# Deformable sampling on one core: one of a step's 72 gathered columns is fetched by SyncE, pixel by pixel

## The reference

```python
offsets = _conv_same(xi, off_w[g], off_b[g])
offsets = offsets.reshape(B, H, W, K * K, 2)
loc = grid[None, :, :, None, :] + kg[None, None, None] + offsets
...
out = wa[..., None] * gather(y0i, x0i) + wb[..., None] * gather(y1i, x0i) + wc[..., None] * gather(y0i, x1i) + wd[..., None] * gather(y1i, x1i)
```

## Time and profile before

| | us |
|---|---|
| three executions, median (lowest, highest) | 12371.41 (12371.2, 12372.86) |
| profiled execution, its own time | 12375.1 |
| its span, first to last instruction | 12373.3 |
| GpSimd busy | 8754.7 (71%) |
| TensorE matmul busy | 7826.9 (63%) |
| VectorE busy | 5178.4 (42%) |
| ScalarE busy | 1654.1 (13%) |
| gathers of GpSimd | 9216 |

### The profile page before, as it was taken

One profiled execution on the slowest core, in us unless ns is written; L12 is line 12 of the kernel. 1 busy time (PEld: TensorE's weight loads), 2 busy tenths in 40 slices (PEclk: granted clock), 3 DMA queues, 4 the chain that ended last, 5 costly groups with the idle time before them and its releaser, 6 DMA issues.

```text
span 12373.3 us, 133594 instructions
## 1 busy us (share of the span) xinstructions
PE 7826.9 (63%) x46178; PEld 6378.0 (52%) x46178; DVE 5178.4 (42%) x6138; ACT 1654.1 (13%) x2837; POOL 8754.7 (71%) x9269
## 2 busy tenths in 40 slices
PE   5766667666467765554457775655457776655488
PEld 3554455545457644444447654444446664444474
DVE  3344444443344444343344444343344444344333
ACT  1011111110011112110001111210001111211015
POOL 3777777777777777777777777777777777777700
PEclk8887778877678877776678877777678887877689
DMA  2333334333244422432234422332224432343271
GB/s 86 102 88 97 111 89 111 105 94 102 73 125 160 130 66 78 115 95 61 67 102 146 167 68 71 100 110 71 57 80 146 171 93 64 92 112 91 62 248 56
DMA packets 878254, 1255.70 MB, mean 101 GB/s; under 512 B 183384, under 2 KB 663320, under 8 KB 860248
## 3 DMA queue, kind: packets, MB, share of 16 engines
q0 software_dynamic: 294912, 604.57, 19.2%
q1 hardware_dynamic: 512216, 601.04, 14.4%
q10 hardware_dynamic: 70912, 47.20, 1.2%
HBM read 1069.49 MB, written 245.50 MB: 106 GB/s over the span
## 4 chain that ended last, share of the span: by engine, by line
POOL 68%; issue 23%; PE 4%; DVE 1%; DMA 1%; ACT 0%; POOLq 0%; PEld 0%; SPq 0%; PEldq 0%; ACTq 0%; DVEq 0%
POOL gathered L471 68%; PE stage L1033 2%; PE stage L926 1%; DVE srow L1561 0%; DMA gathered<-table,idx 0%; PE acc L926 0%; DVE gathered L1554 0%; PE pt L926 0%; POOLq L469 0%; PE wtb L926 0%; PE acc L1175 0%; PEld acc L1175 0%; PE stage L988 0%; POOLq L467 0%; POOLq L477 0%
## 5 line engine op out<-in xcount | busy, mean ns | idle before, releaser
L471 POOL DMA_INDIRECT gathered<-table,idx x9216 | 8730.2, 947 | 2979.2 <-issue 2801.6
L1175 PE MATMUL acc<-stt,room 128*128 128x128 f32 (+1 forms) x30600 | 4372.0, 308 | 234.6 <-ACT stt L901 234.6
L1175 PEld LDWEIGHTS acc<-stt,room 128*128 128x128 f32 (+1 forms) x30600 | 4220.1, 221 | 543.5 <-ACT stt L901 341.5
L1164 PE MATMUL pt<-mat,srow 128*128 128x128 f32 x2048 | 507.2, 394 | 3682.6 <-DVE srow L1561 3682.2
L1164 PEld LDWEIGHTS pt<-mat,srow 128*128 128x128 f32 x2048 | 327.5, 196 | 3882.9 <-DVE srow L1561 3870.6
L1530 DVE COPY idx<-idxn 128x18 uint32<-128x18 uint32 x512 | 98.1, 192 | 5195.8 <-DMA gathered<-table,idx 5187.5
L1561 DVE TENSOR_REDUCE srow<-gathered 128x576 f32<-128x2304 f32 x512 | 2081.1, 4065 | 0.1
L1554 DVE TENSOR_TENSOR gathered<-gathered,wtb 128x2304 f32<-128x2304 f32 x512 | 1306.1, 2551 | 63.0 <-DMA gathered<-table,idx 62.6
L901 ACT ACTIVATE stt<-pt 128x512 f32<-128x512 f32 x512 | 305.9, 597 | 5968.0 <-PE pt L1164 5965.6
L926 PE MATMUL stage<-room,mat 128*128 128x512 f32 (+1 forms) x1360 | 791.4, 712 | 296.6 <-DVE room L1425 70.8
L1033 PE MATMUL stage<-room 128*128 128x128 f32 x7680 | 890.2, 278 | 12.8 <-DMA room<-toep 10.6
(11 more groups left out here) (206 smaller groups left out, 3931.7 us busy)
## 6 DMA issues: line engine op xcount, KB each, us to landing
gathered<-table,idx POOLq DMA_INDIRECT x9216
room<-toep SPq DMA_DIRECT2D x64, 1792.0 KB, 19.0
room<-toep SPq DMA_DIRECT2D x64, 1280.0 KB, 11.5
room<-toep SPq DMA_DIRECT2D x64, 768.0 KB
table<-room SPq DMA_DIRECT2D x64, 512.0 KB, 2.9
toep<-in_taps SPq DMA_DIRECT2D x128, 224.0 KB
toep<-in_taps SPq DMA_DIRECT2D x128, 160.0 KB
room<-in_x SPq DMA_DIRECT2D x4, 4096.0 KB
```

The lines of the kernel that those rows point to most:

```text
L471: nc.gpsimd.indirect_dma_start(gat[r][:, k % K9 * G + k // K9, :], None, table[b].rearrange("(n e) -> n e", e=PAIR), bass.IndirectOffsetOn ...
L1164: ins = nc.tensor.transpose(pt[:, m, :], srow[r % 2][:, m * P:(m + 1) * P], M["ident"])
L1175: ins = nc.tensor.matmul(acc[a][:, 0:W], wk[0:kk, m, dx, block_at * C:block_at * C + P], stt[s][0:kk, m, dx:dx + W], start=start and m == ...
```

## The change

One column of the 72, row `AT_R` = 0 and sample `AT_K` = 17, is no longer gathered by GpSimd, except in step 0. VectorE scales this column's 128 indices to addresses in words and writes them to a tile `column` of 128 x 1 integers. SyncE stores it to DRAM (`column_d`), waits for that, waits until row 0 of the current step is summed, and then fetches the 128 pixels of the next step in 8 chunks of 16: it reads 16 registers from `column_d`, and issues 16 plain DMAs, each of one partition and 128 words, with the register as source address. The chunks stand at times spread over the step, at 1, 2.5, 4 and so on to 11.5. VectorE waits for all 128 of them (`pixels_in`) beside the 17 gathers before it treats row 0. A few semaphores that nothing waited for are dropped as well, and `next_image` drains VectorE where it waited for its own semaphore.

```diff
+AT_R, AT_K = 0, GK - 1
+CHUNK = 16
...
+        column_d = nc.dram_tensor("column_d", [STEPS, P], I32).ap()
...
+        column = sb("column", [P, 1], I32)
...
+        def pixel(p):
+
+            return gat[AT_R][p:p + 1, AT_K % K9 * G + AT_K // K9, :]
...
                 def step(n, b):
                     for r in range(ROWS):
                         v = n * ROWS + r
+                        own = GK if r != AT_R or isinstance(n, int) else AT_K
                         pool.wait_ge(idx_given, v + 1)
                         pool.wait_ge(summed, v + 1)
                         pool.sem_inc(started, 1)
-                        for k in range(GK):
+                        for k in range(own):
...
+                regs = [sp.alloc_register(f"at{j}") for j in range(CHUNK)]
+
+                def fetch_column(n):
+
+                    sp.wait_ge(column_given, n)
+                    sp.dma_start(column_d[ds(n, 1), :].rearrange("o p -> p o"), column[:]).then_inc(column_out, 16)
+                    sp.wait_ge(column_out, 16 * n)
+                    sp.sem_inc(started, 1)
+
+                def fetch_pixels(n, b, q):
+
+                    sp.load(regs, column_d[ds(n, 1), CHUNK * q:CHUNK * (q + 1)])
+                    for j in range(CHUNK):
+                        at = sp.snap(regs[j], min_val=0, max_val=(NPAIR - 2) * PAIR)
+                        sp.dma_start(pixel(CHUNK * q + j), table[b][ds(at, ENTRY)].unsqueeze(0)).then_inc(pixels_in, 16)
+
...
-                    if b == 0:
-                        for k in range(ROWS):
-                            yield 3 * k + 1
+                    last = isinstance(n, int) and n == STEPS - 1
+                    for k in range(ROWS):
+                        yield 3 * k + 1
+                        if b == 0:
                             bands(ROWS * i + k)
+                        if last:
+                            continue
+                        if k == 0:
+                            fetch_column(n + 1)
+                            sp.wait_ge(summed, n * ROWS + AT_R + 1 + ROWS)
+                            sp.sem_inc(started, 1)
+                        per = P // CHUNK // ROWS
+                        for q in range(per * k, per * (k + 1)):
+                            yield 3 * k + 1 + 3 * (q % per) / per
+                            fetch_pixels(n + 1, nb, q)
...
                     then(tt(idxn[:], entry, gbase[:], ALU.add))
+                    if not (isinstance(n, int) and n == 0):
+                        if not (isinstance(n, int) and n == 1):
+                            dve.wait_ge(column_out, 16 * n - 16)
+                        ts(column[:], idxn[:, AT_R, AT_K:AT_K + 1], float(PAIR), None, ALU.mult).then_inc(column_given, 1)
...
-                    dve.wait_ge(landed[r], 16 * GK * (n + 1))
+                    dve.wait_ge(landed[r], 16 * GK + 16 * (AT_K if r == AT_R else GK) * n)
+                    if r == AT_R and not (isinstance(n, int) and n == 0):
+                        dve.wait_ge(pixels_in, 16 * P * n)
                     if give:
                         give_indices(v, r)
```

More of the change, by code:

```diff
@@ L371, in build @@
         table_out = sems("table_out0", "table_out1")
-        off_in, off_used, chain, idx_given, wt_given, moved, started = sems(
-            "off_in", "off_used", "chain", "idx_given", "wt_given", "moved", "started")
+        off_in, off_used, chain, idx_given, wt_given, started = sems(
+            "off_in", "off_used", "chain", "idx_given", "wt_given", "started")
+        column_given, column_out, pixels_in = sems("column_given", "column_out", "pixels_in")
         landed = sems(*(f"landed{r}" for r in range(ROWS)))
@@ L380, in build @@
         bands_out = sems(*(f"bands_out{l}" for l in range(3)))
-        folded, shift_p, ctx_p, gate_p, ctx_s, gate_s = sems("folded", "shift_p", "ctx_p", "gate_p", "ctx_s", "gate_s")
+        shift_p, ctx_p, gate_p, ctx_s, gate_s = sems("shift_p", "ctx_p", "gate_p", "ctx_s", "gate_s")
         cx_out = sems(*(f"cx_out{u}" for u in range(4)))
@@ L474, in step @@
                                 .then_inc(landed[r], 16)
+                step(0, 0)
                 for b in range(NB):
-                    with pool.Fori(b * PER, (b + 1) * PER) as n:
+                    with pool.Fori(max(b * PER, 1), (b + 1) * PER) as n:
                         step(n, b)
@@ L1357, in context_fold @@
                     scale(S["wq"], M["wq"])
-                    scale(gws[:], gw[:]).then_inc(folded, 1)
+                    scale(gws[:], gw[:])
                     yield 13
@@ L1362, in context_fold @@
                     tt(b_q2, PB[2][:, 1:2], V["b_q"], ALU.add)
-                    tt(b_gate2[0:8, :], PB[2][0:8, 2:3], b_gate, ALU.add).then_inc(folded, 1)
+                    tt(b_gate2[0:8, :], PB[2][0:8, 2:3], b_gate, ALU.add)
                 def operands_fold(b, i):
                     yield 11
-                    scale(S["ccen"], M["ccen"]).then_inc(folded, 1)
+                    scale(S["ccen"], M["ccen"])
                     yield 13
                     dve.wait_ge(shift_p, 2 * b + 2)
-                    nc.vector.tensor_copy(b_cen, PB[2][:, 0:1]).then_inc(folded, 1)
+                    nc.vector.tensor_copy(b_cen, PB[2][:, 0:1])
                 def context(b, i):
@@ L1565, in next_image @@
                 def next_image(b):
-                    nc.vector.tensor_copy(base[:], base0[:]).then_inc(moved, 1)
-                    dve.wait_ge(moved, b + 1)
+                    nc.vector.tensor_copy(base[:], base0[:])
+                    dve.drain()
                 def start():
```

## The result

The changed kernel takes 14400.61 us (median of four executions, 14395.13 to 14409.41), the kernel before 12372.01 on the same chip: a ratio of 1.164, with a 95% interval of 1.1625 to 1.1655. It is slower by 2029 us; 14,570 was forecast.

The account below looks back on a forecast made before the run. GpSimd's gathers bound the kernel before, at 90.3 us a step; SyncE's copies, reads and waits would bound the changed one. 12375 + 778 + 1834 - 354 - 56 = 14577, so 14,570 us, range 13,000 to 15,900.

Parts of the forecast that it names:

- What bounds the kernel, and the worth of the gather: GpSimd's gathers bound the kernel before; one gather fewer in each of 127 steps takes off 159 us.
- SyncE becomes the bound, and GpSimd waits for it through VectorE's indices: SyncE's step of 114.6 us in image 0, 109.6 after, exceeds GpSimd's 89.05 and holds VectorE, then GpSimd; 56%.
- A copy at 0.48 us: Each one-pixel copy on SyncE, with register arithmetic, move and boundaries, takes 0.48 us; 128 take 61.4 us a step.
- One memory answer for each read: Each SyncE read, of pointer or 16 words, takes 1.7 us: 27.2 us a looped step, 13.6 in the others.
- The stretch without pixels, 16 us: Each step, SyncE fetches no pixel for 16 us while offsets load, indices are made and row 0 is summed.
- SyncE keeps up: Rival: the column's fetch fits into GpSimd's 89.05 us step, GpSimd stays the bound, 12216 us, about 12,230; 12%.
- One memory answer a chunk: Rival: SyncE's pointer reads are nearly free, so pixels take 75 us a step and the time is 13,200 us; 15%.
- The DMA engine is the limit: Rival: one-partition copies use a single DMA engine and back up; at 0.6 us a copy 16,500 us; 16% with dearer reads.
- the ring: Not in the prediction; later reading: pixels, their row, other engines' work behind it, SyncE's stores for them, the next pixels.

Follow-up runs that it names:

- experiment 3: The changed kernel with 17 gathers in row 0 and no column work on SyncE, the column's samples left out: 12215.72 us, ratio 0.9872.
- experiment 1: The changed kernel with the 16 registers read only once, before the first pixels, and all copies kept: 12220.01 us, ratio 0.9876.
- experiment 7: The changed kernel with a column of row 3 instead of row 0, fetched in the step using it, and one row of `column_d`: 13338.12 us, ratio 1.0756.

## Why the prediction was right

**What bounds the kernel, and the worth of the gather.** Right: 159 us were priced, and without any work on SyncE the time fell by 158 (experiment 3).

**SyncE becomes the bound, and GpSimd waits for it through VectorE's indices.** Right in mechanism, by the chain, by GpSimd's waits, and by experiment 1. One link was named wrong: VectorE was to wait for the pixels at the index copy of row 0, and it never did there. It waited for the load of offsets at its first index operation, 4433 us in all, because SyncE's program has that load behind the last pixel and VectorE's has the indices ahead of row 0. The mean step was forecast at (778 + 1834 - 354) / 127 + 90.3 = 108.1 us and is 106.8; the sum is 175 us too high (14577 for 14401.8 profiled). That it is so close is in part luck, on errors that cancel.

**A copy at 0.48 us.** 0.40 measured, below my lower end. The copy itself takes 0.22 us for the 0.30 that I took from the store of 64 words to `table`; the boundaries were as read. The copies of a step take 53.1 us for the 61.4 forecast, so this term was 8.3 us too much.

**One memory answer for each read.** The sum held, 3.4 us a chunk forecast and 1.10 + 1.96 and the boundaries, 3.3, measured; over a mean step 24.4 us forecast and 25.6 measured. Its form did not: a read costs by begun groups of 8 words, so 16 words cost nearly twice what the pointer costs. The Trainium skill's 200 ns a register (Runtime: NRT & Kernel Launch, section Instruction fetch mechanics) is not what these runs show, which is 0.12 us a word from 16 words on. The Trainium skill's floor of 600 ns (DMA: Bandwidth & Descriptors, section Latency and other measured facts) is below the median of 1.10 us here. The lower bound of the range for this mechanism was added up wrong: at 2.4 us a chunk the same sum gives about 13,660 us (14,570 less 101 x 8 and 26 x 4), not 13,900.

**The stretch without pixels, 16 us.** 19.7 measured (7.3 + 14.5 from the load of offsets to the first pixel, less 3.3 for the first reads, and 1.2 ahead of the load). The step that failed is that the column's store is hidden by row 0's product and sum. I gave it 1.7 us to land; it takes 10.0 in the mean, and it ended SyncE's wait in 105 of 127 steps, row 0's sum in 22.

**Not foreseen:** the loop's jump back, 1.6 us a step in the mean. So 8.3 us too much for the copies stand against 3.7 too little for the stretch, 1.6 for the jump, 1.2 for the reads and some 0.5 for SyncE's own copies and waits: together 1.3 us a step too much.

**The rivals.** *SyncE keeps up* was decided by the reads, as its condition said: at 0 us a chunk it does (12,220), at 2.1 it does not (13,639). *One memory answer a chunk* fell with the reads' durations. *The DMA engine is the limit* fell with experiment 1; the longest copy of 16,256 was 0.65 us. The packets of SyncE's queue say something on how a copy is spread, which the prediction had from no row: they went from 512,216 to 563,016, which is 3 for each copy and 16 for each store of the column. So a copy is not spread over 16 engines. Which engine moves it, no view shows. What I had not among the rivals is the ring: I took the 16 us as something that offsets and row 0 cause, and row 3 left as long a turn.

## What to carry to other kernels

Before work goes to an idle engine, add its issue time to the waits that its own program puts in front of the work: an idle share is room only if the work can be issued during it. A buffer that is filled and freed once a step can make a ring of the engine that fills it and the engines that empty it, and the ring's length is then a step's floor. Moving the column from row 0 to row 3 left the time at 14,381 us for 14,401, so before such a move, add up what will stand between the last fill and the next in the new place. Whether a second buffer opens the ring was not shown here. A register loaded from memory held SyncE for 1.1 us and more, so count these reads and the hidden ones of addresses, and make the addresses constant: that alone gave 761 us.

## What the runs showed of the hardware that I had not expected

A read of registers from DRAM by SyncE took 1.10 us for 2 or 8 words, 1.96 for 16 and 3.75 for 32, in the median. A store of 128 words of 4 bytes, one from each partition, to DRAM took 7.0 us to land in the step shown and held SyncE 10.0 us in the mean, up to 23.1. The issue of a one-partition copy takes 0.22 us, against 0.33 for the load of offsets.

At a loop's jump back SyncE stood for 2.4 to 3.4 us in the changed kernel, against 0.10 to 0.27 in the kernel before, and for up to 9.0 in experiment 7. The instruction queue of the changed kernel moved 676 packets, against 75:

```profile
q14 instruction: 676, 5.54, 0.1%
```

In the traces a pass through one of its step loops runs 435 to 531 instructions on SyncE, against 13 to 109 before. The Trainium skill (Runtime: NRT & Kernel Launch, section Instruction fetch mechanics) says that a taken branch to a place outside the two pages at hand must first fetch the page. The trace agrees with that, by the packets and the 73 jumps; that the fetch alone fills the 2.4 to 3.4 us is not shown.
